# Squared key norms taken from the Gram matrix's diagonal on GpSimd, and the load of x issued earlier on SyncE

## The reference, cut to what matters

```python
lam = sigmoid(lam_logit); beta = eta * (1.0 - lam) / d            # d = 16
x_act = tanh(x); static_out = einsum('bld,ed->ble', x_act, W)
q = k = to_heads(x_act); v = to_heads(static_out)
# per head and token:  S = lam * S
#                      u = beta * (v - S^T k);  S = S + k u^T;  o = S^T q
y = static_out + o_dyn                                            # o of all heads
x = layernorm(x + layernorm(y) * ln_gamma + ln_beta)
x = layernorm(x + W_down(silu(W_gate x) * (W_up x)))
```

## Time and profile before

| | |
|---|---|
| median of 3 runs | 1711.97 us (1702.58 to 1717.01) |
| the profiled execution | 1699.24 us, of which the span from first to last instruction is 1697.4 us |
| mean granted TensorE clock | 0.881 of full speed |
| busy share of the span | PE 80%, DVE 80%, ACT 66%, POOL 50% |
| one step in the middle of the run | about 49 us |
| DMA | 190.98 MB in 701325 packets, mean 113 GB/s |

### The profile page before, as it was taken

The page is one execution under the profiler, slowest core; times in us unless marked ns, Lnnn a source line. Parts: engine busy times, 40 slices in busy tenths (PEclk is TensorE's granted clock), DMA queues, the critical chain, the costliest instruction groups (busy, mean ns, idle before and its releaser), DMA issues.

```text
span 1697.4 us, 53741 instructions
## 1 busy us (share of the span) xinstructions
PE 1362.5 (80%) x21032; PEld 1062.5 (63%) x21032; DVE 1352.3 (80%) x3461; ACT 1115.9 (66%) x2357; POOL 842.8 (50%) x1106
## 2 busy tenths in 40 slices
PE   4357888888888888888888888887888888888764
PEld 3345676666666666666666666666666666666542
DVE  5588888888888888888888888888788788888841
ACT  3335777667767776676777677766667677676544
POOL 6124455555544655454455555445555544555542
PEclk9557889989989998898899899898999899899877
DMA  4556445565655555566455566654565555455200
GB/s 121 118 109 119 106 122 121 119 124 114 130 118 120 122 122 116 114 123 130 110 120 119 120 125 117 125 116 115 115 116 121 114 131 117 118 117 120 52 23 25
DMA packets 701325, 190.98 MB, mean 113 GB/s; under 512 B 620944, under 2 KB 688528, under 8 KB 701072
## 3 DMA queue, kind: packets, MB, share of 16 engines
q1 hardware_dynamic: 701072, 187.56, 52.1%
HBM read 103.55 MB, written 67.11 MB: 101 GB/s over the span
## 4 chain that ended last, share of the span: by engine, by line
DVE 29%; SPq 18%; PE 16%; DMA 13%; issue 12%; ACT 8%; POOL 4%; ACTq 0%; POOLq 0%; DVEq 0%
SPq L1059 8%; DMA xa<-L_attn_x 6%; PE pc L182 6%; DMA scr_g<-gs 5%; PE pg L253 4%; DVE tt L451 4%; SPq L1072 4%; PE pu L253 4%; DVE gs L443 3%; DVE gate L495 3%; SPq L994 3%; DVE xt L406 2%; DVE x1lo L488 2%; DVE U L382 2%; DVE R L377 2%
## 5 line engine op out<-in xcount | busy, mean ns | idle before, releaser
L953 POOL TENSOR_TENSOR hlo<-gate,hhi 128x512 f16<-128x512 f32 x192 | 264.0, 1385 | 357.0 <-ACT hhi L783 354.9
L182 PE MATMUL pc<-R,tb 128*128 128x32 f16 x4096 | 158.1, 186 | 119.3 <-DVE R L372 117.3
L182 PEld LDWEIGHTS pc<-R,tb 128*128 128x128 f16 x4096 | 146.7, 118 | 139.8 <-DVE R L372 137.7
L182 PE MATMUL pc<-U,kb 128*128 128x32 f16 x4096 | 158.9, 188 | 85.3 <-DVE U L382 85.1
L182 PEld LDWEIGHTS pc<-U,kb 128*128 128x128 f16 x4096 | 146.9, 118 | 114.7 <-DVE U L382 114.6
L182 PEld LDWEIGHTS pc<-S,e 128*128 128x128 f16 x4096 | 150.1, 118 | 67.9 <-DVE S L399 64.4
L182 PE MATMUL pc<-S,e 128*128 128x32 f16 x4096 | 157.1, 186 | 41.5 <-DVE S L399 41.4
L279 PE MATMUL pd<-wd_t,hhi 128*128 128x256 f16 x768 | 174.5, 274 | 7.5 <-POOL hlo L953 5.1
L279 PE MATMUL pd<-wd_t,hlo 128*128 128x256 f16 x768 | 174.1, 274 | 0.0
L216 PEld LDWEIGHTS pf<-xb,e 128*128 128x128 f16 x4096 | 153.8, 118 | 31.5 <-DMA e<-scr_x 16.3
L216 PE MATMUL pf<-xb,e 128*128 128x32 f16 x4096 | 156.3, 191 | 17.5 <-DMA e<-scr_x 15.9
(11 more groups left out here) (132 smaller groups left out, 3222.4 us busy)
## 6 DMA issues: line engine op xcount, KB each, us to landing
xa<-L_attn_x SPq DMA_DIRECT2D x128, 128.0 KB
scr_x<-xt SPq DMA_DIRECT2D x64, 256.0 KB, 2.1
xb<-scr_x SPq DMA_DIRECT2D x256, 64.0 KB, 2.9
e<-scr_x SPq DMA_DIRECT2D x256, 64.0 KB, 3.7
scr_g<-gs SPq DMA_DIRECT2D x32, 512.0 KB, 3.5
gh<-scr_g SPq DMA_DIRECT2D x32, 512.0 KB, 3.3
kb<-k SPq DMA_DIRECT2D x512, 32.0 KB, 2.3
scr_t<-t SPq DMA_DIRECT2D x64, 256.0 KB, 3.6
```

What stands on the lines that cost most here:

```text
L182: last = pe.matmul(pc2[:, :, cols], stationary(h, a), moving[:, :, cols], start=a == 0, stop=a == 1)
L953: pool.tensor_tensor(hlo[:, t, :], gate[:, t % 2, :], hhi[:, t, :], ALU.subtract).then_inc(SEM["hl"], 1)
```

## The change

The diagonal of the Gram matrix is the squared norm of each key. The mask's diagonal, zero before, becomes one, so that DVE's L428 leaves the squared norms on the diagonal of `gh`. POOL scales them into a small tile `nd` ([128, 16, 4]; a new instruction, `pool_key_norms`) and SP turns them through DRAM: one store `nd` to `scr_n` (`sp_store_norms`) and one load `scr_n` to `nb` (`sp_load_norms`, 128 partitions of 16 x 4 values, 16 bytes contiguous in DRAM for each head). `nb` now has four buffers. ACT's square (L682), DVE's sums (L418) and DVE's scaling (L423) are gone. The load of x now waits for the rounded keys (`k16`) in place of the sums, and stands directly behind the store of `gs`, ahead of the `gh` load and the second half of `tb`. POOL's unit diagonal goes behind `pool_bias(s - 2, p, 2)`.

```diff
--- before.py
+++ after.py
@@ -66,13 +66,14 @@
 
         xa = sb("xa", [P, NW, D])
         k16 = sb("k16", [P, 2, H, DH, 2, 2], F16)
-        nb = sb("nb", [P, 2, NW, H])
+        nb = sb("nb", [P, 4, H, NW])
         xt = sb("xt", [P, 2, 2, B, C, NW], F16)
         E = [sb(f"e{p}", [P, 2, H, B, C, NW], F16) for p in range(2)]
         gs = sb("gs", [P, H, C, NW])
         gh = sb("gh", [P, C, C, NW])
         xb = sb("xb", [P, 2, H, C, NW], F16)
         tt = sb("tt", [P, C, C, NW])
+        nd = sb("nd", [P, C, NW])
         tmp = gs[:, 0:C - 1, :, :]
         t16 = sb("t16", [P, 2, C, C, 2, 2], F16)
         tb = sb("tb", [P, 2, H, B, C, 2, 2], F16)
@@ -117,11 +118,12 @@
 
         scr_x = nc.dram_tensor("scr_x", [2, 2, P, B, T], F16).ap()
         scr_g = nc.dram_tensor("scr_g", [H, B, C, T], F32).ap()
+        scr_n = nc.dram_tensor("scr_n", [H, B, C, NW], F32).ap()
         scr_t = nc.dram_tensor("scr_t", [2, H, B, C, T], F16).ap()
 
         PER = dict(
             xin=64, xa=1, xtp=2, xth=2, xt=2,
-            sq=1, nr=1, nb=1, k16h=2, k16=2,
+            nd=1, kd=16, nb=16, k16h=2, k16=2,
             xtd=32, e=128, xb=128, vp=2, v=2,
             gp=4, ga=4, g=4, gd=16, gh=16,
             tf=29, tc=1, t1=1,
@@ -412,17 +414,6 @@
             dve.scalar_tensor_tensor(dst[:, 1], src, kcol[:, 0:1], dst[:, 0], ALU.mult, ALU.subtract)\
                .then_inc(SEM["k16"], 1)
 
-        def dve_square_sums(dve, q, p):
-            dve.wait_ge(SEM["y1"], n_of("y1", q - 2))
-            dve.wait_ge(SEM["sq"], n_of("sq", q))
-            dve.tensor_reduce(nb[:, p, :, :], xa[:, :, :].rearrange("p n (h k) -> p n h k", h=H),
-                              AX.X, ALU.add).then_inc(SEM["nr"], 1)
-
-        def dve_key_norms(dve, q, p):
-            dve.wait_ge(SEM["nr"], n_of("nr", q))
-            dve.tensor_scalar(nb[:, p, :, :], nb[:, p, :, :], sc[:, BETAR:BETAR + 1], -0.5 / RS,
-                              ALU.mult, ALU.add).then_inc(SEM["nb"], 1)
-
         def dve_mask_gram(dve, q, p):
             dve.wait_ge(SEM["gh"], n_of("gh", q))
             dve.tensor_tensor(gh[:, :, :, :], gh[:, :, :, :],
@@ -513,7 +504,6 @@
                 dve_multiply(dve, s - 2, p, 1)
                 dve_multiply(dve, s - 2, p, 2)
             if live(s):
-                dve_key_norms(dve, s, p)
                 dve_store_inverse(dve, s, p, 1)
             if live(s - 1):
                 dve_statistics(dve, s - 1, 1 - p, 3)
@@ -570,9 +560,6 @@
                 dve_rest_high(dve, s, p, 1)
                 dve_rest_sum(dve, s, p, 1)
                 dve_rest_low(dve, s, p, 1)
-            if live(s + 1):
-                dve_square_sums(dve, s + 1, 1 - p)
-            if live(s):
                 dve_update_high(dve, s, p, 1)
                 dve_update_low(dve, s, p, 1)
                 dve_statistics(dve, s, p, 0)
@@ -676,11 +663,6 @@
             act.wait_ge(SEM["xin"], n_of("xin", q))
             act.activation(xa[:, :, :], xa[:, :, :], ACT.Tanh).then_inc(SEM["xa"], 1)
 
-        def act_square(act, q, p):
-            act.wait_ge(SEM["k16"], n_of("k16", q))
-            act.wait_ge(SEM["xtp"], n_of("xtp", q))
-            act.activation(xa[:, :, :], xa[:, :, :], ACT.Square).then_inc(SEM["sq"], 1)
-
         def act_transpose_keys(act, q, p, half):
             src = pf[half][:, :].rearrange("p (n t) -> p t n", n=NW)
             dst = xt[:, half].rearrange("p z b i n -> p z (b i) n")
@@ -742,7 +724,7 @@
             if n == 0:
                 act.wait_ge(SEM[f"mq{z}"], n_of(f"mq{z}", q))
                 if z == 2 and q == NS - 1:
-                    act.wait_ge(SEM["nr"], n_of("nr", q))
+                    act.wait_ge(SEM["xtp"], n_of("xtp", q))
                     act.wait_ge(SEM["k16"], n_of("k16", q))
                 elif z == 3 and q < NS - 1:
                     act.wait_ge(SEM["res"], n_of("res", q + 1))
@@ -826,8 +808,6 @@
                 act_scale_keys(act, s + 1, 1 - p, 1)
             if live(s):
                 act_decay(act, s, p, 1)
-            if live(s + 1):
-                act_square(act, s + 1, 1 - p)
             if live(s - 2):
                 act_variance(act, s - 2, p, 3, 0)
             if live(s):
@@ -903,6 +883,12 @@
             one = powers[:, 0:1, None].to_broadcast([P, C, NW])
             pool.tensor_tensor(tt[:, :, :, :].rearrange("p j i n -> p (j i) n")[:, 0:C * C:C + 1, :],
                                one, one, ALU.mult).then_inc(SEM["t1"], 1)
+
+        def pool_key_norms(pool, q, p):
+            pool.wait_ge(SEM["tf"], n_of("tf", q, 1))
+            pool.wait_ge(SEM["kd"], n_of("kd", q - 1))
+            pool.tensor_scalar(nd[:, :, :], gh[:, :, :, :].rearrange("p i j n -> p (i j) n")[:, 0:C * C:C + 1, :],
+                               sc[:, BETAR:BETAR + 1], -0.5 / RS, ALU.mult, ALU.add).then_inc(SEM["nd"], 1)
 
         def pool_attention_out(pool, q, p, w):
             pool.wait_ge(SEM["u"], n_of("u", q, w + 1))
@@ -914,7 +900,7 @@
             pool.wait_ge(SEM["y0"], n_of("y0", q, w + 1))
             pool.tensor_tensor(bu[:, :].rearrange("p (h d) -> p h d", h=H),
                                bu[:, :].rearrange("p (h d) -> p h d", h=H),
-                               nb[:, p, w, :, None].to_broadcast([P, H, DH]), ALU.mult)\
+                               nb[:, q % 4, :, w, None].to_broadcast([P, H, DH]), ALU.mult)\
                 .then_inc(SEM["y1"], 1)
             pool.wait_ge(SEM["y1"], n_of("y1", q, w + 1))
             pool.tensor_tensor(v[:, p, w, :], v[:, p, w, :], bu[:, :], ALU.add).then_inc(SEM["y"], 1)
@@ -960,9 +946,11 @@
             if live(s - 1):
                 pool_attention_out(pool, s - 1, 1 - p, 1)
             if live(s):
+                pool_key_norms(pool, s, p)
+            if live(s - 2):
+                pool_bias(pool, s - 2, p, 2)
+            if live(s):
                 pool_unit_diagonal(pool, s, p)
-            if live(s - 2):
-                pool_bias(pool, s - 2, p, 2)
             if live(s - 1):
                 pool_attention_out(pool, s - 1, 1 - p, 2)
             if live(s - 2):
@@ -989,7 +977,7 @@
         def sp_load_x(sp, q, p):
             sp.wait_ge(SEM["xtp"], n_of("xtp", q - 1))
             sp.sem_inc(s_hop, 1)
-            sp.wait_ge(SEM["nr"], n_of("nr", q - 1))
+            sp.wait_ge(SEM["k16"], n_of("k16", q - 1))
             for n in range(NW):
                 sp.dma_start(xa[:, n, :], x[:, q * T + n * C:q * T + (n + 1) * C, :]).then_inc(SEM["xin"], 16)
 
@@ -1037,8 +1025,23 @@
             sp.wait_ge(SEM["gd"], n_of("gd", q))
             sp.sem_inc(s_hop, 1)
             sp.wait_ge(SEM["tf"], n_of("tf", q - 1))
+            sp.sem_inc(s_hop, 1)
+            sp.wait_ge(SEM["nd"], n_of("nd", q - 1))
             sp.dma_start(gh[:, :, :, :].rearrange("p i j n -> p (i j n)"),
                          scr_g.rearrange("h b i t -> (h b) (i t)")).then_inc(SEM["gh"], 16)
+
+        def sp_store_norms(sp, q, p):
+            sp.wait_ge(SEM["nd"], n_of("nd", q))
+            sp.sem_inc(s_hop, 1)
+            sp.wait_ge(SEM["nb"], n_of("nb", q - 1))
+            sp.dma_start(scr_n.rearrange("h b i n -> (h b) (i n)"), nd[:, :, :].rearrange("p i n -> p (i n)"))\
+              .then_inc(SEM["kd"], 16)
+
+        def sp_load_norms(sp, q, p):
+            sp.wait_ge(SEM["kd"], n_of("kd", q))
+            sp.sem_inc(s_hop, 1)
+            sp.wait_ge(SEM["y1"], n_of("y1", q - 4))
+            sp.dma_start(nb[:, q % 4], scr_n.rearrange("h b i n -> (b i) h n")).then_inc(SEM["nb"], 16)
 
         def sp_store_inverse(sp, q, p, g):
             sp.wait_ge(SEM["t16"], n_of("t16", q, g + 1))
@@ -1091,10 +1094,14 @@
 
         def sp_step(sp, s, p):
             if live(s + 1):
+                sp_store_norms(sp, s + 1, 1 - p)
                 sp_load_kb(sp, s + 1, 1 - p, 0)
             if later(s + 2):
                 sp_store_keys(sp, s + 2, p, 0)
                 sp_store_keys(sp, s + 2, p, 1)
+            if live(s + 1):
+                sp_load_norms(sp, s + 1, 1 - p)
+            if later(s + 2):
                 sp_spread_packed_keys(sp, s + 2, p)
                 sp_spread_keys(sp, s + 2, p)
             if live(s + 1):
@@ -1107,11 +1114,12 @@
                 sp_load_kb(sp, s + 1, 1 - p, 1)
             if live(s + 2):
                 sp_store_gram(sp, s + 2, p)
-                sp_load_gram(sp, s + 2, p)
-            if live(s + 1):
-                sp_load_inverse(sp, s + 1, 1 - p, 1)
             if later(s + 3):
                 sp_load_x(sp, s + 3, 1 - p)
+            if live(s + 2):
+                sp_load_gram(sp, s + 2, p)
+            if live(s + 1):
+                sp_load_inverse(sp, s + 1, 1 - p, 1)
             if live(s - 1):
                 sp_store_out(sp, s - 1, 1 - p)
 
@@ -1143,7 +1151,7 @@
         for t in range(NHT):
             jobs.append(([wd32[a][:, t * P:(t + 1) * P] for a in range(2)], wd_t[:, t, :]))
         NJ = len(jobs)
-        N_SETUP = 1 + 8 + 2 * C + 7 + 1 + (C - 1)
```

(7 more changed lines are left out.)

2 lines of the change are left out of this document (1 added, 1 removed).

## The result

The changed kernel takes 1735.33 us (median, 1732.23 to 1751.67) against 1712.18 us before: ratio 1.0162, 95% interval 1.0083 to 1.0240. The forecast of 1694 us is wrong, and so is its sign. The profiled execution took 1738.03 us, its span is 1736.2 us, 38.8 us longer than that of the kernel before.

What follows compares the result with a forecast made beforehand. It took the kernel to be a loop of waits that no engine carries; 18 + 1 + 2 - 3 = 18 us off the profiled 1699.24 gave 1681, or 1694 us in the median's scale, range 1676 to 1716.

Steps and rivals of the forecast that it cites:

- x earlier: x issued some 4.3 us earlier covers tanh's longest wait of 2.0 us; worth 18.7 us at most, taken as 18.
- What x is moved past: In SP's list, gh load (1.7 us spare) and second tb half (1.9 us spare): cost taken as nothing.
- first rival: Gram load late at DVE's mask behind x's bytes: 37 us lost against 18 gained, 1731 in median's scale; chance 0.12.
- step B: Profiled step of the kernel before: tanh waited 1.96 us for x, released 6.9 us after x's issue at 1167.80.
- DVE's sums and scaling, ACT's square: Work removed from DVE and ACT: sums and square worth nothing, scaling 1 us, at most 8 us.
- SP's two issues: The norms' store and load in SP's list: 0.1 us a step, 3 us lost in all; bounds nothing and 58 us.
- second rival: Gain goes into SP's list: xb, E and the inverse's stores slip, 19 us lost against 18; same time, 1712; chance 0.22.
- middle case: Price of the norms' load if 0.6 us a step meets no slack in SP's list: 19 us lost.
- TensorE's clock: Less PE idling in the third round may keep 2.4 GHz longer: worth 0 to 14 us, taken as 2 gained.
- The landmarks: Trace signs listed beforehand; wrong if DVE idles before the mask for gh, SP's inverse waits vanish, or clock well above 0.881.

Runs made afterwards that it cites:

- e7: e2 without the norms' path (no POOL scaling, no norm DMAs, nb a constant zero, output incomplete): 1693.05 us, ratio 0.9879 to the kernel before.
- e11: Kernel before with norms kept on ACT and DVE, square in its own tile, x loaded between gh and tb's second half: 1694.09 us, ratio 0.9913.
- e4: Changed kernel with x's four DMAs loading half the bytes, all ahead of gh (output not the reference's): 1694.57 us, ratio 0.9904 to the kernel before.
- e8: e2 with both norm DMAs issued from ACT's list in place of SP's: 1701.56 us, ratio 0.9951 to the kernel before.
- e1: Changed kernel with the load of x back behind tb's second half, norms still through DRAM: 1717.36 us, ratio 1.0030 to the kernel before.
- e2: Changed kernel with x issued between the gh load and tb's second half: 1701.12 us, ratio 0.9954 to the kernel before.
- e6: Kernel before with only x moved ahead of the gh load, still waiting for the sums of squares: 1838.94 us, ratio 1.0740.
- e9: e2 with the load of the norms made twice, into two tiles: 1722.64 us, ratio 1.0082 to the kernel before.

## Why the prediction was wrong

**x earlier: right.** The wait of the tanh is gone and its link is 2.65 us, as the forecast asked. e7 and e11 show about the worth that it gave: 0.9 to 1.2%.

**What x is moved past: wrong, and this is the step that failed.** I let `gh` go at 821.3, added the 3.3 us of the earlier trace rows and found 1.7 us spare: "Cost nothing, as long as x's bytes don't hold `gh` up". But 3.3 us is the landing of a `gh` load with nothing heavy ahead of it in the queues. The order had changed, and the duration from the old order was carried over. Behind x it is 6.4 us (e4, with SP's list unchanged and half of x's bytes: 4.5), so 821.3 + 6.4 = 827.7 against the mask at 826.26: 1.4 us late in place of 1.7 early. The trace of before had the figure that mattered: x takes 6.9 us from its first issue to its release, and I used it in the first rival alone.

**The first rival was the outcome.** It forecast `gh` 1.2 us behind the mask, 1718 us of profiled time and 1731 in the median's scale; measured 1.16 us in the step shown, 1738.03 and 1735.33. Its two terms hold, 39 us lost and 20 won. The profiled execution is 20 us over it, with 17 of them in the stretch of the lower clock; that the median is within 4 us is in part luck. I gave it 0.12 because in step B x had `tb` ahead and the output stores beside it. That was a guess at the reason for the 6.9 us. The changed kernel's trace shows x slow with nothing else in flight: 0.145 MB a us on 46.5% of the engines, so 3.6 us for its 0.52 MB.

**DVE's sums and scaling, ACT's square: right at nearly nothing.** e11 keeps all three and is as fast, within the intervals, as e7, which has none (0.9913 against 0.9879).

**SP's two issues: the size was off.** I put 3 us for the path and priced its load at 1.6 us of all engines. By e8's packets the load takes 1.2 us (and it moves 32 KB, not the 128 that I wrote; its price went by the count), and in SP's wait it is free, as I had placed it. The path as a whole costs more: e1, with x in its old place, is 5 us over the kernel before by the ratio, and e7 is 8 us under e2. Which of scaling and store takes it is not settled. The second rival named the right slack: a second load used it up and cost 22 us. That this is near the 19 us of the middle case is luck, since the middle case was the price of one load on the engines and the second one cost SP's time.

**TensorE's clock: wrong sign.** I took 2 us of gain. The mean granted clock went from 0.881 to 0.857 and PE's busy time from 1362.5 to 1376.7 us for the same 21032 matmuls; the feed-forward's products grew by 16.1 us, and the link that holds half of them by 0.55 us a step, 17 us in all, at a clock of 0.80 there in place of 0.87. With the late `gh` (39 us) and the early x (20 us) that makes 36 of the 38.8 us. Why the clock fell there stays open. It is not simply that PE idles longer in the third round: in e6 it idles far longer there, and its feed-forward's products took the 604.3 us of before.

**The landmarks.** Of those that would show the forecast wrong, the first was named exactly: an idle time of DVE ahead of the mask, released by `gh`'s load.

## What to carry to other kernels

When a transfer is moved ahead of another, the landing time of the one that is passed is no longer that of the old trace: add the bytes still ahead of it when it is issued, at the rate that the moved one reaches alone (here that came within 0.7 us). Check what share of the engines the moved one keeps busy alone: x, at 46.5%, needed 3.6 us for its 0.52 MB. And look for the place in the list that gives the moved transfer nearly all of its lead without passing the urgent one: here one position further back was worth 2%.

## What the runs showed of the hardware that I had not expected

A 512 KB load landed 3.3 us after its issue behind nothing, 6.4 us behind 512 KB cut with 8 sequences outermost, and 3.8 us behind the same 512 KB cut with 16 rows outermost and issued over a longer time. A second load of 2048 pieces directly behind the first held SP for 1.28 us at its issue, the first for 0.43 (e9). Pieces of 16 bytes cost the transfer engines less than those of 128 bytes (9.2 ns, averaged with the store's 256-byte pieces, against 12.7 ns). By the Trainium skill, "DMA: Bandwidth & Descriptors", section "Specifications", transfers under 512 B fall below line rate; the trace agrees that these cost mostly by count: an eighth of the bytes costs 9.2 in place of 12.7 ns. And still 2048 of them were free where SP had 1.4 us to spare.
